# A graph-attention layer on one core: matches of ring places from squared distances in place of turned one-hot matrices

## The chip, the cores and the metric

The kernel runs on 1 core of one Trainium2 chip. The time is the device time of one execution in microseconds (us), the median of several runs. Within the core TensorE (PE; PEld is its weight load), VectorE (DVE), ScalarE (ACT) and GpSimd (POOL) work beside each other, each in the order of its own program, and meet through semaphores; SyncE (SP) issues most DMA transfers. A trailing q (DVEq, POOLq) names an engine's sequencer.

## The reference

12500 nodes of 128 numbers, 212500 edges with 64 numbers each, sorted by destination; 4 heads of 32 numbers.

```python
h = relu(layernorm(x)); n = (h @ W_node.T).reshape(12500, 4, 32)
e = (edge_attr_64 @ W_edge.T).reshape(212500, 4, 32)
att = sum(concat([n[src], n[dst], e], -1) * a, -1)      # edge x head
att = where(att > 0, att, 0.2 * att)
m = maximum(segment_max(att, dst), 0.0)
ex = exp(att - m[dst])
denom = segment_sum(ex, dst) + (212500 - deg)[:, None] * exp(-m)
out = x + segment_sum((ex / denom[dst])[:, :, None] * n[src], dst)
```

## The kernel before

**Prologue.** TensorE turns and projects the node rows (98 windows of 128 nodes); ScalarE writes the projected rows and the source score of each head, 132 numbers a node, to the table `h_table` in memory (`rows_out`, stored by SP's `store_rows`). `s2`, the destination score, stays in SBUF. The gathers of the first 5 groups fetch raw node rows instead (also shown as L487), so that work starts before the table is complete. VectorE then makes flags of where the destination changes from edge to edge (L611), and tables that say for each step which two neighbouring windows its edges fall into (up to L698): `base`, `in_this`, `in_next`, `keep`, and the records from which each engine reads its addresses at run time (`dve_rec`, `act_rec`, `sp_rec`).

**Main loop.** 52 supers of 4 groups of 1024 edges (8 tiles of 128). `walk` (L87) runs a pair of steps twice for each super, so a step is a group. For each super POOL issues 32 indirect gathers (L487) of 128 table rows each, 4 supers ahead in a ring `gath` of 16 slots. A super's first group waits for `released` (DVE, L870: the super four back is done with), and each of its other groups for `stepped` (DVE, L850), which counts finished steps.

The destinations of a step lie within 256 nodes, and `ring` maps them to 128 ring places. A step k takes:

1. DVE: sum of the destination scores (L791), scores with slope (L796 to L814), then `one_hot` of step k+1 (L727: edges on partitions, 1 where the edge's destination is at that ring place, 8 tiles of 128x128 in bf16), then `normalise` (L880 to L886) and the weighted rows `vals` (L835).
2. ACT: exponentials of the maxima before (L1055, L1056), of the scores (L1036, L1037), two small blocks of live scores (`live_s2`, L1078), `transposed` (L1084), `factors` (L1063), `widened` (L1090: the one-hot to f32).
3. PE, `turn_one_hot` of step k+1 (L1210): 8 transposes of `onehot_b` into the bank `bank_t`, started by DVE's L727. ACT's `transposed` copies the bank to `onehot_t` (places on partitions), and PE's `spread_s2` (L1220) multiplies `onehot_t` with the live scores: every edge of step k+1 gets its destination's score, which L791 of step k+1 adds up.
4. PE, the products of step k (L1243): 8 tiles of one-hot times `vals`, f32, shown as 16 matmuls. The next step's `merge` on DVE (L755 to L764) takes them up, then ACT's `factors` and DVE's `rescale` (L772, L775), which ends with `stepped`.

Beside that, PE makes the edge scores of the next super behind the products of a super's second step (`both_products`, L1185, 32 matmuls). Around the fourth step: DVE `z_columns` (L708), PE `turn_z` (L1193), two scans on DVE (L715, L719) for the maximum of each destination, PE `maxima` (L1203), and two copies by ACT (L1014, L1021), for which the next super's L791 waits.

In the rest of the text S is `spread_s2`, T `turn_one_hot`, P the products, Z `both_products`, each with its step's number where one is meant.

What sets the order is the program of each engine alone; there is no scheduler. The lines that wait on PE before S and P:

```python
wait(e, s_sl, count); wait(e, s_sn, count); wait(e, s_e, count)   # spread_s2: live scores, transposed
wait(e, s_v, s_1); wait(e, s_mc, s_1); wait(e, s_de, s_1); wait(e, s_of, s_1)   # products: vals, exp, widened
```

## Time and profile before

| what | value |
|---|---|
| median of 3 runs | 2956.02 us (2949.07 to 2960.83) |
| the profiled execution, its own time | 2958.49 us |
| its span in the trace | 2956.7 us |
| mean granted TensorE clock | 0.618 of full speed |
| PE, DVE, ACT, POOL busy | 1394.2, 1558.5, 796.3, 1576.9 us |
| DMA | 224.74 MB, mean 76 GB/s |

No engine is busy for much over half of the span. The busy times are sums over stages, so the waits by stage have to be read: `<-DVEq L850` behind a POOL row says that a gather started when DVE's sequencer reached L850, `<-remote` that the releasing event isn't among the records of the engines' own instructions, or came later than the modelled end of the instruction that gave it. The record of a TensorE group gives where its matmuls began and a modelled end; when others learnt of that end is seen in the row of the engine that waited.

### The profile page before, as it was taken

To read this page: it belongs to the slowest core of one execution; us is meant where nothing else is said; L and a number is where in the kernel's file an instruction comes from. 1 tells how busy PE (TensorE), PEld (TensorE's weight loads), DVE (VectorE), ACT (ScalarE), POOL (GpSimd) and SP (SyncE) were. 2 spreads that over 40 slices of the span, in tenths; PEclk is the share of its full clock that TensorE was granted. 3 is DMA by queue.
4 is the path that set the end of the run, shared out by engine and by line. 5 is a ranking of instruction groups with operands and counts; after the bars stand their busy time and mean duration, and the time that the engine had idled before them with its cause. 6 is when DMAs were issued, how large, how long until landed. Compare 5 with 4: busy or idle time off the path is not lost.

```text
span 2956.7 us, 39019 instructions
## 1 busy us (share of the span) xinstructions
PE 1394.2 (47%) x9599; PEld 1292.3 (44%) x9600; DVE 1558.5 (53%) x4449; ACT 796.3 (27%) x2329; POOL 1576.9 (53%) x1674
## 2 busy tenths in 40 slices
PE   4424544544545445444455464454544544544465
PEld 4414444434445444344344353444433433534455
DVE  4345554554545555545555445455454555454568
ACT  4412222222222222222222222222222222222233
POOL 6525555555555555555655555556555555555530
PEclk7656665656655656656556556565565666565667
DMA  7352322222222223222222232222222222222220
GB/s 210 81 185 64 81 66 63 78 69 64 78 66 80 67 64 80 67 65 78 68 70 73 67 80 67 65 77 69 66 77 65 79 67 65 81 66 64 80 67 22
DMA packets 119885, 224.74 MB, mean 76 GB/s; under 512 B 40373, under 2 KB 80181, under 8 KB 113093
## 3 DMA queue, kind: packets, MB, share of 16 engines
q0 software_dynamic: 53440, 113.99, 16.5%
q1 hardware_dynamic: 65565, 110.07, 11.5%
q10 hardware_dynamic: 848, 0.35, 0.1%
q8 instruction: 10, 0.16, 0.0%
q14 instruction: 22, 0.18, 0.0%
HBM read 180.28 MB, written 43.98 MB: 76 GB/s over the span
## 4 chain that ended last, share of the span: by engine, by line
another core or an unknown queue 38%; DVE 23%; issue 17%; PE 12%; ACT 5%; DVEq 3%; ACTq 1%; DMA 0%; SPq 0%
PE bank_z L1185 5%; DVE vals L835 5%; DVE bank_rn L715 4%; DVE rows_mem L719 3%; PE bank_w L1243 3%; DVE s_sum L791 2%; ACT onehot_bits L1084 2%; PE bank_rn L1203 2%; PE bank_t L1210 1%; DVE lk L804 1%; DVEq L80 1%; ACT s_live L1078 1%; ACTq L80 1%; DVE den L880 1%
## 5 line engine op out<-in xcount | busy, mean ns | idle before, releaser
L487 POOL DMA_INDIRECT gath<-h_table,idx x1621 | 1531.7, 945 | 1260.1 <-issue 458.1
L1084 ACT COPY onehot_bits<-bank_t 128x1024 bf16<-128x1024 bf16 x209 | 211.5, 1012 | 1279.3 <-remote 915.9
L1220 PE MATMUL bank_s<-s_live,onehot_bits 128*128 128x24 bf16 x1672 | 76.1, 179 | 842.4 <-ACT onehot_bits L1084 759.5
L1220 PEld LDWEIGHTS bank_s<-s_live,onehot_bits 128*128 128x128 bf16 x1672 | 61.1, 102 | 891.4 <-issue 891.4
L1243 PE MATMUL bank_p<-vals,onehot 128*128 128x137 f32 x1664 | 404.2, 435 | 0.3
L1243 PEld LDWEIGHTS bank_p<-vals,onehot 128*128 128x128 f32 x1664 | 377.4, 328 | 4.9 <-DVE vals L835 0.2
L1210 PE MATMUL bank_t<-ident_b,onehot_bits 128*128 128x128 bf16 x1672 | 199.2, 293 | 358.6 <-DVE onehot_bits L727 310.6
L1210 PEld LDWEIGHTS bank_t<-ident_b,onehot_bits 128*128 128x128 bf16 x1672 | 163.5, 139 | 381.9 <-DVE onehot_bits L727 325.3
L1243 PE MATMUL bank_w<-vals,onehot 128*128 128x137 f32 x1664 | 320.8, 367 | 0.0
L1243 PEld LDWEIGHTS bank_w<-vals,onehot 128*128 128x128 f32 x1664 | 298.4, 266 | 0.0
L727 DVE SCALAR_TENSOR_TENSOR onehot_bits<-bank_w,tables,zz 128x1024 bf16 (+1 forms) x209 | 268.3, 1284 | 27.4 <-issue 12.9
L1185 PEld LDWEIGHTS bank_z<-w_edge_bd,ef 128*128 128x128 f32 x1664 | 266.6, 254 | 20.8 <-issue 11.7
L1185 PE MATMUL bank_z<-w_edge_bd,ef 128*128 128x8 f32 x1664 | 261.6, 298 | 21.1 <-issue 12.3
L772 DVE SCALAR_TENSOR_TENSOR live<-live,tables,ab 128x132 f32<-128x132 f32 x209 | 73.3, 351 | 335.8 <-ACT ab L1063 335.8
L755 DVE SCALAR_TENSOR_TENSOR m_run<-m_run,tables,bank_p 128x4 f32<-128x4 f32 x104 | 20.7, 199 | 420.8 <-remote 420.8
L715 DVE TENSOR_TENSOR_SCAN bank_rn<-flag_rows,bank_rn 16x1024 f32<-16x1024 bf16 x52 | 118.7, 2282 | 210.3 <-remote 206.3
L1090 ACT CAST onehot<-onehot_bits 128x1024 f32<-128x1024 bf16 x208 | 214.6, 1032 | 0.0
L791 DVE TENSOR_REDUCE s_sum<-bank_s 128x32 f32<-128x192 f32 x208 | 73.3, 352 | 196.2 <-remote 128.1
L1203 PE MATMUL bank_rn<-ident,rows_mem 16*128 16x16 f32 x416 | 50.1, 256 | 213.9 <-DVE rows_mem L719 213.9
L1063 ACT ACTIVATE ab<-ab_log 128x8 f32<-128x8 f32 x209 | 44.0, 210 | 392.3 <-DVE ab_log L762 380.3
L1203 PEld LDWEIGHTS bank_rn<-ident,rows_mem 16*128 16x128 f32 x416 | 46.0, 206 | 223.2 <-issue 223.2
L835 DVE TENSOR_TENSOR vals<-gath,bank_p 128x1024 f32<-128x1024 f32 x104 | 126.3, 1215 | 0.0
(167 smaller groups left out, 1851.2 us busy)
## 6 DMA issues: line engine op xcount, KB each, us to landing
ef<-in_edges SPq DMA_DIRECT2D x52, 1024.0 KB
out_x<-x_all SPq DMA_DIRECT2D x210, 128.0 KB
gath<-h_table,idx POOLq DMA_INDIRECT x1621
x_all<-in_x SPq DMA_DIRECT2D x14, 448.0 KB, 6.1
out_x<-x_all SPq DMA_DIRECT2D x14, 448.0 KB
h_table<-gath SPq DMA_DIRECT2D x12, 462.0 KB
resets<-ef SPq DMA_DIRECT2D x8, 416.0 KB
flag_rows<-resets SPq DMA_DIRECT2D x52, 64.0 KB
```

What stands on the lines that cost most here:

```text
L487: e.indirect_dma_start(gath[:, q * GPS + g, t * ROW:(t + 1) * ROW], None, table, bass.IndirectOffsetOnAxis(idx[:, q, g * TILES + t:g * TIL ...
L715: e.tensor_tensor_scan(rows, first_rows, rows, NEG, ALU.add, ALU.max).then_inc(scan_f, 1)
L727: e.scalar_tensor_tensor(out=onehot_b[buf][:, :, :], in0=ring_p[:, bass.ds(offset, P)].rearrange("p (a j) -> p a j", a=1) .to_broadcast([P ...
L791: e.tensor_reduce(s2_sum[:, :].rearrange("p (t h) -> p t h", h=HEADS), s2e[q].rearrange("p (t k h) -> p t h k", k=6, h=HEADS), AX_X, ALU.a ...
L835: e.tensor_tensor(vh[:, :, :, 0:HD], gath[:, bass.ds(slot, 1), :].rearrange("p a (t c) -> p (a t) c", c=ROW)[:, :, 0:DIM].rearrange("p t ( ...
L1084: e.copy(onehot_t[:, :, :], bank_t[:, :].bitcast(BF16).rearrange("p (t c) -> p t c", c=P)).then_inc(s_e, 1)
L1090: e.copy(onehot[buf][:, :, :], onehot_b[buf][:, :, :]).then_inc(s_of, 1)
L1185: ins = e.matmul(z_edge[:, 2 * k:2 * k + 2, t, :], ef[:, k, t * P:(t + 1) * P], w_edge_bd[:, :], start=True, stop=True)
L1203: ins = e.transpose(z_back[:, t * GH:(t + 1) * GH], z_rows[:, t * P:(t + 1) * P], ident[0:GH, 0:GH])
L1210: ins = e.transpose(bank_t[:, :].bitcast(BF16)[:, t * P:(t + 1) * P], onehot_b[buf][:, t, :], ident_b[:, :])
L1220: ins = e.matmul(s2e[buf][:, t * S2W:(t + 1) * S2W], onehot_t[:, t, :], s2_live[:, :], start=True, stop=True)
L1243: ins = e.matmul(half_p[q], onehot[q][:, t, :], vals[q][:, t, :], start=(t == 0), stop=(t == TILES - 1))
```

## The change

The transposed one-hot of a step is no longer made from the one-hot. For a ring place p and a destination d, both split in two parts (bits 112 and bits 15, `HIGH` and `LOW`), (ph-dh)^2 + (pl-dl)^2 is zero where they match and at least 1 where they don't. `distances` makes this sum as a matmul over 18 rows: `terms_sb` holds for each edge of a super dh^2, dl^2, dh and dl of its four groups (rows 4g to 4g+3) and two rows of ones; `place_sb` holds for each of the four groups' positions 1, 1, -2ph and -2pl, and in the last two rows ph^2 and pl^2. `place_sb` stands in a block of its own for each group, chosen at run time by `sel`; the columns of `terms_sb` by `at`, both read from a new table `pe_rec`. The result fills `bank_t` (128x512, f32) with half of a step's 1024 edges, so each step takes two, `distances(0)` and `distances(1)`, called D0 and D1 here. ACT's `matched(0)` and `matched(1)` (L1205) write `onehot_t` from them as relu(1 - distance), 128x512 each, in place of `transposed`. The one-hot itself (DVE L727) and `widened` stay.

The distances are made two steps ahead: step k's part of the program runs S of step k+1, D0 of k+2, P of k, D1 of k+2. D1 waits until `matched(0)` has emptied the bank; ACT's `matched(1)` waits for D1 and stands ahead of the next step's `den_parts` and exponentials. `turn_z` comes first in the fourth step, and `maxima` and Z come behind D1.

The terms are made in the prologue and kept in memory (`dst_terms`); SP fetches 32 KB of them for each super (`load_terms`, a ring of four) at a super's first pair, and PE waits for them at the start of a super (`d_terms`).

In the prologue the destinations (`dst_rows`, `dst_next`, `dst_here`) are no longer fetched early, but behind the stores of the projected rows, the first of them on SP where SP had it between loads of x and the others on SP where POOL issued them; they arrive as integers and ACT casts them into banks or `dst_f` (8 casts), DVE splits them in bits (2 operations on 104x2048) and ACT makes squares and casts of them (4 operations on 104x2048) which ACT stores by 4 DMAs; two operations set the terms' rows of ones. VectorE makes the place rows at its start (10 small operations; they go to memory and come back by 5 loads) and `pe_rec` (8 more behind the tables). The comparison for the flags is in 3 pieces, the one for `is_last` in 4. The 14 copies of x to the output move ahead of the resets on SP. POOL waits for the stored terms before the gathers of the first turn's last super. `ident_b` is gone.

```diff
 def pair(u, ...):                                     # PE
-                    turn_one_hot(1 - q, s_2)
                     if beside[q][0]:
                         beside[q][0]()
-                    spread_s2(1 - q, s_2)
+                    spread_s2(1 - q, s_2, (h4, h6)[q])
+                    ahead = (sel_a, at_a) if q == 0 else (sel_b, at_b)
+                    distances(0, *ahead)
...
                     ins.then_inc(s_b, 1)
+                    distances(1, *ahead, (h5, h7)[q])
...
-                ins = e.transpose(bank_t[:, :].bitcast(BF16)[:, t * P:(t + 1) * P],
-                                  onehot_b[buf][:, t, :], ident_b[:, :])
-            ins.then_inc(s_t, 1)
+            def distances(k, sel, at, count=None):
+                if count is not None:
+                    wait(e, s_e, count)
+                e.matmul(bank_t[:, :], place_sb[:, bass.ds(sel, P)],
+                         terms_sb[:, bass.ds(at + k * 512, 512)], start=True, stop=True
+                         ).then_inc(s_t, 1)
...
             def beside(b):
-                return ((None, None, None),
+                return ((lambda: e.wait_ge(d_terms, b * 16 + 16), None, None),
...
 def pair(u, ...):                                     # ACT
                     live_s2((w_b, w_c)[q], s + 3)
-                    transposed(s_2)
+                    matched(0, (h5, h7)[q])
                     factors(s, s_1)
                     widened(1 - q, s, s_2)
+                    matched(1, (h6, h8)[q])
...
-                e.copy(onehot_t[:, :, :], bank_t[:, :].bitcast(BF16).rearrange(
-                    "p (t c) -> p t c", c=P)).then_inc(s_e, 1)
+                e.activation(onehot_t[:, k * 4:(k + 1) * 4, :], bank_t[:, :].rearrange(
+                    "p (t c) -> p t c", c=P), ACT.Relu, bias=one[:, :], scale=-1.0
+                    ).then_inc(s_e, 1)
...
 SP, prologue
-                if c == 10:
-                    e.dma_start(dst_rows, dst_groups).then_inc(d_rows, 16)
...
+            e.dma_start(dst_rows, dst_groups).then_inc(d_rows, 16)
+            e.dma_start(dst_next, dst_l[:, 1, :, :]).then_inc(d_dst, 16)
+            e.wait_ge(d_store, 16 * CHUNKS)
+            wait(e, n_s2, 2)
+            e.dma_start(dst_here, dst_l[:, 0, :, :]).then_inc(d_dst, 16)
...
 POOL, first gathers
-                if g == 1:
-                    e.dma_start(dst_f[:, :, :], dst_l[:, 0, :, :]).then_inc(d_dst, 16)
-                    e.dma_start(dst_next, dst_l[:, 1, :, :]).then_inc(d_dst, 16)
...
             for q in range(1, RING):
+                if q == RING - 1:
+                    e.wait_ge(d_terms_out, 16 * TERMS)
...
 ACT, prologue
+            for bank, g, at, n in turned_rows:
+                e.copy(bank[0:GROUPS // 2, 0:n], dst_rows[:, g, at:at + n]).then_inc(n_turned, 1)
...
+            e.copy(dst_f[:, :, :], dst_here).then_inc(n_turned, 1)
...
+            wait(e, n_bits, 2)
+            for k, (part, func) in enumerate(((dst_rows, ACT.Square), (dst_low, ACT.Square),
+                                              (dst_rows, ACT.Copy), (dst_low, ACT.Copy))):
+                e.activation(terms_out[k], part, func).then_inc(n_terms, 1)
+            wait(e, n_terms, TERMS)
+            for k in range(TERMS):
+                e.dma_start(terms[:, k, :].rearrange("(p g) e -> p g e", g=2), terms_out[k]
+                            ).then_inc(d_terms_out, 16)
```

TensorE in the loop over supers, first pair of a super, in the kernel before (L1210 is T, L1220 S, L1243 P, L1185 Z):

```order
L1210 MATMUL bank_t<-ident_b,onehot_bits 128x128 x8
L1220 MATMUL bank_s<-s_live,onehot_bits 128x24 x8
L282 REGISTER_ALU
L1243 MATMUL bank_p<-vals,onehot 128x137 x8
L282 REGISTER_ALU
L1210 MATMUL bank_t<-ident_b,onehot_bits 128x128 x8
L1220 MATMUL bank_s<-s_live,onehot_bits 128x24 x8
L1243 MATMUL bank_w<-vals,onehot 128x137 x8
L1182 ISA
L282 REGISTER_ALU
L1185 MATMUL bank_z<-w_edge_bd,ef 128x2x4 x16
```

And the same place of the changed kernel (L1346 is S, L1336 D0 and D1, L1377 P, L1310 Z):

```order
L1346 MATMUL bank_s<-s_live,onehot_bits 128x24 x8
L1336 ISA
L1336 MATMUL bank_t<-rows_mem,place_mem 128x512
L305 REGISTER_ALU
L1377 MATMUL bank_p<-vals,onehot 128x137 x8
L305 REGISTER_ALU
L1336 ISA
L1336 MATMUL bank_t<-rows_mem,place_mem 128x512
L305 REGISTER_ALU x2
L1346 MATMUL bank_s<-s_live,onehot_bits 128x24 x8
L1336 ISA
L1336 MATMUL bank_t<-rows_mem,place_mem 128x512
```

The 8 transposes ahead of S are gone; one matmul stands between S and P, and one behind P, where S of the next step follows.

ScalarE at the end of a pair's first step, before (L1078 is `live_s2`, L1084 `transposed`, L1063 `factors`, L1090 `widened`, L1055 and L1056 `den_parts`, L1036 the next step's exponentials):

```order
L1078 ACTIVATE s_live<-s,tables 128x12
L282 REGISTER_ALU
L1084 COPY onehot_bits<-bank_t 128x1024
L1063 ACTIVATE ab<-ab_log 128x8
L1090 CAST onehot<-onehot_bits 128x1024
L1055 ACTIVATE unseen<-m_run 128x4
L1056 ACTIVATE others<-live 128x1
L1036 ACTIVATE bank_w<-dd 128x32
```

And of the changed kernel (L1205 is `matched`, L1183 `factors`, L1212 `widened`):

```order
L1198 ACTIVATE s_live<-s,tables 128x12
L305 ISA
L1205 ACTIVATE onehot_bits<-bank_t,one 128x512
L1183 ACTIVATE ab<-ab_log 128x8
L305 REGISTER_ALU
L1212 CAST onehot<-onehot_bits 128x1024
L305 REGISTER_ALU
L1205 ACTIVATE onehot_bits<-bank_t,one 128x512
L1175 ACTIVATE unseen<-m_run 128x4
L1176 ACTIVATE others<-live 128x1
L1155 ACTIVATE bank_w<-dd 128x32
```

The copy is split in two, and the second half stands behind `widened` and ahead of all that belongs to the next step.

## Rows read from the trace of the kernel before

**Rows 1.** The page: busy time by engine; the chain that ended last.

```profile
PE 1394.2 (47%) x9599; PEld 1292.3 (44%) x9600; DVE 1558.5 (53%) x4449; ACT 796.3 (27%) x2329; POOL 1576.9 (53%) x1674
...
another core or an unknown queue 38%; DVE 23%; issue 17%; PE 12%; ACT 5%; DVEq 3%; ACTq 1%; DMA 0%; SPq 0%
```

**Rows 2.** POOL's waits by releaser, 223.72 to 2844.25: total, times, longest.

```profile
POOL gath L487 <- DVEq L850: 437.8, 96, 8.8
POOL gath L487 <- DVEq L870: 285.3, 48, 8.0
```

**Rows 3.** Windows: us, busy by engine (instructions), PE clock, DMA share, GB/s.

```profile
1025.28:1050.03 24.75, 7.24 (x51) 6.42 (x52) 12.07 (x39) 7.31 (x20) 15.08 (x16) 0.50 0.23 56
1050.03:1063.64 13.61, 8.64 (x65) 8.35 (x65) 5.93 (x19) 3.23 (x13) 7.54 (x8) 0.63 0.30 60
1063.64:1079.90 16.26, 9.73 (x64) 9.00 (x62) 10.18 (x22) 3.49 (x12) 7.55 (x9) 0.71 0.31 99
223.72:2844.25 2620.53, 1240.21 (x8545) 1150.69 (x8544) 1365.32 (x3831) 679.85 (x1990) 1464.28 (x1552) 0.61 0.27 71
2858.39:2890.75 32.36, 21.82 (x176) 20.17 (x176) 27.94 (x80) 14.14 (x41) 0.00 (x0) 0.71 0.15 51
```

**Rows 4.** Timeline 1024 to 1051: start, us, engine, operation, [idle before <-releaser].

```profile
1030.42 0.37 PE L1220 MATMUL bank_s<-s_live,onehot_bits 128*128 128x24 bf16 x8 [1.19 <-issue]
...
1030.75 3.99 PE L1243 MATMUL bank_p<-vals,onehot 128*128 128x137 f32 x16
...
1034.49 0.36 DVE L791 TENSOR_REDUCE s_sum<-bank_s 128x32 f32<-128x192 f32 x1 [2.94 <-remote]
...
1037.46 1.03 PE L1210 MATMUL bank_t<-ident_b,onehot_bits 128*128 128x128 bf16 x8 [2.71 <-DVE onehot_bits L727]
...
1043.99 0.94 POOL L487 DMA_INDIRECT gath<-h_table,idx  x1 [0.30 <-issue]
1048.02 1.01 ACT L1084 COPY onehot_bits<-bank_t 128x1024 bf16<-128x1024 bf16 x1 [11.47 <-remote]
1048.04 0.22 DVE L755 SCALAR_TENSOR_TENSOR m_run<-m_run,tables,bank_p 128x4 f32<-128x4 f32 x1 [8.84 <-remote]
```

**Rows 5.** Timeline 1050 to 1064: the run of eight gathers behind the edge products.

```profile
1053.19 3.75 PE L1185 MATMUL bank_z<-w_edge_bd,ef 128*128 128x8 f32 x32
...
1058.87 0.94 POOL L487 DMA_INDIRECT gath<-h_table,idx  x1 [0.30 <-issue]
1061.63 1.01 ACT L1084 COPY onehot_bits<-bank_t 128x1024 bf16<-128x1024 bf16 x1 [9.87 <-remote]
...
1063.64 0.94 POOL L487 DMA_INDIRECT gath<-h_table,idx  x1 [3.83 <-DVEq L850]
```

**Rows 6.** Timeline 1062 to 1082: the step with the scans.

```profile
1067.44 1.04 PE L1193 MATMUL bank_rn<-ident,z_cols 128*16 128x128 f32 x8
...
1072.98 2.28 DVE L715 TENSOR_TENSOR_SCAN bank_rn<-flag_rows,bank_rn 16x1024 f32<-16x1024 bf16 x1 [4.94 <-remote]
...
1079.90 0.36 DVE L791 TENSOR_REDUCE s_sum<-bank_s 128x32 f32<-128x192 f32 x1 [0.77 <-ACT zz L1021]
```

**Rows 7.** Timeline 2857 to 2872: a step of the tail, with no gathers issued.

```profile
2861.86 1.21 DVE L835 TENSOR_TENSOR vals<-gath,bank_p 128x1024 f32<-128x1024 f32 x1
...
2863.54 0.37 PE L1220 MATMUL bank_s<-s_live,onehot_bits 128*128 128x24 bf16 x8 [1.19 <-ACT onehot_bits L1084]
...
2864.56 0.35 DVE L791 TENSOR_REDUCE s_sum<-bank_s 128x32 f32<-128x192 f32 x1
```

**Rows 8.** Groups of 0 to 216 us: count, busy, mean ns, idle before.

```profile
L975 ACT ACTIVATE ef<-bank_w 128x512 f32<-128x512 f32 x13 | 7.9, 630 | 15.4 <-remote 11.7 <-PE bank_w L1137 3.7
```

**Rows 9.** Timeline 160 to 216: the prologue's last gather, flags, the first restart.

```profile
164.65 0.94 POOL L487 DMA_INDIRECT gath<-h_table,idx  x1 [0.30 <-issue]
...
173.20 2.29 DVE L611 TENSOR_TENSOR ef<-rows_mem 104x2046 bf16<-104x2046 int32 x1 [56.70 <-remote]
...
205.36 0.94 POOL L487 DMA_INDIRECT gath<-h_table,idx  x1 [39.77 <-DVEq L698]
```

More of the change, by code:

```diff
@@ L515, in _ @@
             chain(e.memset(eps[:, :], 4.0 * EPS))
+            chain(e.memset(one[:, :], 1.0))
+            e.memset(place_sb, 0.0).then_inc(n_place, 1)
+            chain(e.memset(place_row[:, 0:2, :], 1.0))
+            wait(e, n_const, 2)
+            chain(e.tensor_copy(place_high, ring[32:33, 0:P]))
+            chain(e.tensor_single_scalar(place_low, place_high, LOW, op=ALU.bitwise_and))
+            chain(e.tensor_single_scalar(place_high, place_high, HIGH, op=ALU.bitwise_and))
+            for k, part in enumerate((place_high, place_low)):
+                times, square = place_row[:, 2 + k, :], place_row[:, TERMS + k, :]
+                chain(e.tensor_scalar(times, part, -2.0, None, ALU.mult))
+                ins = e.scalar_tensor_tensor(out=square, in0=times, scalar=0.25, in1=times,
+                                             op0=ALU.mult, op1=ALU.mult)
+                if k == 0:
+                    chain(ins)
+            ins.then_inc(n_place, 1)
             def statistics(c):
```

171 lines of the change are left out of this document (135 added, 36 removed).

## The prediction

> **What bounds the kernel now.** I read the busy times first: no engine is busy for more than 53% of the span [rows 1], and the chain that ended last puts 38% on events that no record explains. So waits bound it. Who waits? The only engine whose rate gives a floor for the loop is POOL: a gather each 1.25 us (0.94 and 0.30 between [rows 4]), 32 to a super, 40 us. The loop takes longer: 1552 gathers in 2620.53 us [rows 3] are 48.5 supers of 54.03 us. POOL waits in it for DVE's L850 (437.8 us) and L870 (285.3 us) [rows 2], 14.9 us a super. The remaining question is why DVE is late.
>
> A super has three phases, one to each run of gathers: 24.75 us with 16, 13.61 with 8, and a third with 8 that takes 54.03 - 24.75 - 13.61 = 15.67 us in the mean (the one shown 16.26) [rows 3]. In the tail, where no gathers are issued, four steps take 32.36 us with the same matmuls [rows 3]. A single hand-over shows the same: S is issued at 2863.54 and DVE uses it at 2864.56, 1.0 us later [rows 7]; under gathers S(1) is issued at 1030.42 and used at 1034.49, 4.1 us later [rows 4]. P(1), issued at 1030.75 with a modelled length of 3.99, is seen by DVE's L755 only at 1048.04, after 8.84 us idle, and T(2), issued at 1037.46, by ACT at 1048.02 after 11.47 idle [rows 4]: two groups issued 7 us apart come free together, 4.0 us after the start of the run's last gather (1043.99), 22.7 us after the run's first. In the run of 8, Z and T come free at 1061.63, 2.8 us after the last gather (1058.87), 11.6 after the first [rows 5]. Then ACT and DVE work for 2.0 us until POOL's next gather at 1050.03 and at 1063.64. So **the kernel is a loop: a run of gathers holds back TensorE's completions, and these hold back the next run.** Within a run matmuls come back slowly: S(1)'s 8 took 4.07 us, 0.51 each. P(1)'s 16 were not back 13.55 us after S(1), so at least 0.85 each, if they weren't simply held to the end.
>
> Here a rule speaks against my reading. The Trainium skill, "SBUF — State Buffer", section "Who interferes with whom", says that DMA never contends with a compute engine and that TensorE never waits on anyone, having ports of its own. By it the lateness would be TensorE's own. The two ends at a fixed distance from the last gather speak against it; it has a rival below.
>
> **The change, part by part.** PE has 176 matmuls a super [rows 3] (32 S, 32 T, 64 P, 32 Z, 8 `turn_z`, 8 `maxima`); T goes, and 8 D come: 152. In the tail T costs the path little (S, not T, is waited for), so what counts is where T stood in a run.
>
> *Phase 1.* P(1) no longer stands behind T and S, which were made a step earlier; it needs `vals`(1) alone, so I put it 4.85 us after the run's start instead of 5.47. P(1) and D1(3) are 17 matmuls. At 0.51 each they are back at 13.5, at 0.85 at 19.3; I take 0.85, since P is the like of P. Behind D1(3) stand in ACT's order `matched(1)` (0.63, the 128x512 activation [rows 8]), the exponentials of step 2 (two of about 0.2, as the small operations of rows 4) and `live_s2`; for these waits DVE's `vals` (1.21 [rows 7]), and for that PE's P(2) and DVE's `merge`. With D1(3) at 19.3, `vals` ends at 22. Then S(3) and D0(4), 9 matmuls, are issued after 20 and held to the run's end, 22.7. From there before: copy 1.01, then `factors` and `rescale`, 1.0 more, 24.75. Now the copy is a `matched(0)` of 0.63: **24.35, -0.4**.
>
> *Phase 2.* S(4) and D0(5) are held to the end of the run behind Z (32 matmuls) as T was. `matched(0)` for the copy, and S needs no turn through T: 13.1, **-0.5**.
>
> *Phase 3.* Before, `turn_z` is issued at 1067.44 behind T, and the first scan starts at 1072.98 after 4.94 idle, 9.34 us into the run; L791 of the next super follows 6.92 later, and POOL 16.26 after the run's start [rows 6]. T's 8 matmuls are gone from in front of it: at 0.45 each, a little under S(1)'s 0.51, 3.6 us, so the scan starts at 5.7. Floor for this term: none of it, if all is held to the end. With the scan at 5.7 the scans are over at 10.3. Now the next thing is late: P(4) and D1(6), ahead of `maxima`, come at the run's end, 11.5. `maxima` and ACT's copies took what the two scans leave of the 6.92, 6.92 - 2 x 2.28 = 2.4, of which I take 2.0, since the hand-over from the scan is long past and `matched(1)` lies beside `maxima`: 13.5 against 15.67, **-2.2** (0 to -2.8).
>
> Sum -3.1 us a super, times 48.5: **-150 us**.
>
> *The other edits of the loop.* PE's load of `pe_rec` twice a super, has no row; PE idles 1.19 us ahead of S with its present loads [rows 4], which bounds one load, and it lies in PE's wait for `vals`: 0, and if that cover is gone up to 1 us a super. SP's 32 KB a super stand in SP's queue ahead of nothing urgent (DMA is busy 0.27 of the time [rows 3]); PE waits for terms fetched a super ahead: nothing. ACT does two activations of 0.63 for one copy of 1.01, +0.25 a step, in an engine that idles over 8 us in each phase: nothing beyond what stands above.
>
> *Prologue.* The last gather of the first batch starts at 164.65, L611 starts at 173.20 after 56.7 us idle, and POOL starts again at 205.36 with 39.77 idle, released by the last table's operation [rows 9]. What lies on these 32 us is added in full: the casts of `dst_rows` ahead of the flags (3 casts, 1.0 + 0.6 + 0.6 by the length of 128x512 at 0.63 [rows 8]), 2 bitwise operations of 104x2048 at L611's 2.29 [rows 9], 8 small ones at 0.2 for `pe_rec`, some sequencing: 2.2 + 4.6 + 1.6 + 1.2 = 9.6, taken as **+10**. Bounds: 0, if the casts were done before ACT's work is waited for, and +20, if the fetch of `dst_rows` behind the row stores lands late, since nothing hides a DMA there. The first super's distances wait for terms that ACT makes in 4 operations of about 2.3 and stores: beside POOL's gathers of the second and third super, 70 us, for which the new wait of POOL comes too late to matter. The 14 copies of x, now ahead of the resets on SP, may put 0 to 3 us on them.
>
> *Tail.* Without gathers the path loses the T that hid anyway and gains the order P(k), D1, `matched(1)`, exponentials of k+1, which puts P on the path to the next exponentials: 0 to 3 us a super, three supers: **+2**.
>
> Sum: -150 + 10 + 2 = -138. 2958.49 - 138 = 2820.5; the median of before lies 2.5 below its profiled execution: **2818 us**. Own range 2780 to 2900 (phase 3 between half and all of its term, a gain of 1 us in phase 1, prologue to +20).
>
> **The rivals.**
> 1. *No change.* D1(3) is held to the end of run 1 like T(2) was. This is so if matmuls come back at over (22.7 - 4.85)/17 = 1.05 us each. Then all of step 2's exponentials, `vals` and `merge` come after 22.7: matched(1) 0.6, exponentials and waits 0.7, `vals` 1.2, merge, factors, rescale 1.6: 26.8, +2.1. Phase 2 -0.3, phase 3 -2.1: -0.3 x 48.5 + 12 = -3: **2953 us**. For it: P(1) did come exactly with T(2) [rows 4]. Against: S(1) came within the run.
> 2. *Slower.* The same, and `turn_z` isn't earlier either: it is held to 9.3 whatever stands before it, and `matched(1)` adds 0.6 there. +2.1 - 0.3 + 0.6 = +2.4 x 48.5 + 12 = +128: **3084 us**. It decides from the point where P's 16 matmuls and D1 outlast the run: the wait on D1 turns P, which was beside the next step's exponentials, into what they wait for.
> 3. *Faster.* All in the run comes back at S(1)'s 0.51: P(1) and D1(3) at 13.5, S(3) out at 15.0, with D0(4) back at 19.6, POOL's release at 21.2: -3.6; phase 2 -0.5, phase 3 -2.8: -6.9 x 48.5 + 12 = -323: **2633 us**. Against: the 13.55 us of P(1).
> 4. *Lateness is TensorE's own*, by the count of matmuls, not by gathers: 24 of 176 fewer, 14% of POOL's 723 us of waits: -100 + 10: **2866 us**. Against it stands the tail, where the same matmuls are prompt. The Trainium skill's rule named above would lead to this case.
>
> **How the numbers follow.** Main 0.40, no change 0.20, slower 0.20, faster 0.10, TensorE's own 0.10. About 0.5% is what a measurement of this kernel can tell from no change (2941 to 2971). Faster: main, faster and own lateness 0.60, less 0.05 for the main case's weak end, plus 0.05 from the no-change case's spread: 0.60. Within: 0.05 + 0.12 = 0.17. Slower: 0.20 + 0.03 = 0.23. The range goes from 2700, which takes in part of the faster case, to 3010, for the mild part of the slower one (+0.6 to +2.4 a super): it leaves out some 0.06 below and 0.13 above.
>
> **What would show it.** Right, if in the changed kernel the first scan (L715 of before) starts some 6 us into its run rather than 9.3, and the third phase lasts 13.5; if D1(3)'s `matched(1)` comes at most 20 us into the run of 16, and that phase lasts 24.4; if POOL restarts after the prologue at 213 to 218. Wrong, if `matched(1)` of the run of 16 starts at its end, 22.7 (rivals 1 and 2), or if the grouping of gathers in runs of 16, 8 and 8 changes: another grouping makes each phase's sum void. The prices rest on one super's rows, and above all on what P's matmuls do inside a run, which the trace of before bounds only from below.

## The result, and the profile after

| what | before | changed |
|---|---|---|
| median of 17 runs | 2964.85 us | 2990.5 us |
| range of the runs | 2949.07 to 2974.17 | 2950.83 to 3024.38 |
| the profiled execution | 2958.49 us | 3013.91 us |

The ratio of the compared runs is 1.0053 (95% interval 1.003 to 1.0076): slower by half a percent, where 5% faster was forecast. It leaves out, as slow, the 7 of the changed kernel's 17 runs that lie over 1.5% above its fastest; the medians of all runs are 0.9% apart. The changed kernel's runs spread far more than those of before, and its profiled execution lies 23 us above its median; so I take from this trace how it works, and split the time by a pair of traces from one other chip, below.

The page of the changed kernel (busy times; the chain; two groups, with busy and mean ns, then idle time before them and its releaser):

```profile
PE 1497.7 (50%) x8347; PEld 1259.0 (42%) x8348; DVE 1566.5 (52%) x4473; ACT 888.7 (30%) x2554; POOL 1572.2 (52%) x1672
...
another core or an unknown queue 43%; PE 20%; issue 15%; DVE 10%; ACT 7%; ACTq 3%; DVEq 2%; DMA 0%; POOL 0%; SPq 0%; POOLq 0%
...
L1205 ACT ACTIVATE onehot_bits<-bank_t,one 128x512 bf16<-128x512 f32 x420 | 288.5, 687 | 1749.7 <-remote 1211.9
...
L804 DVE TENSOR_TENSOR_SCAN bank_rn<-flag_mem,bank_rn 16x1024 f32<-16x1024 bf16 x52 | 118.4, 2277 | 3.1 <-issue 2.8
```

The same scan's line on the page of the kernel before:

```profile
L715 DVE TENSOR_TENSOR_SCAN bank_rn<-flag_rows,bank_rn 16x1024 f32<-16x1024 bf16 x52 | 118.7, 2282 | 210.3 <-remote 206.3
```

VectorE stood idle ahead of a super's first scan (L804, L715 of before), for `turn_z`, 210.3 us in all in the kernel before; here 3.1 us are left. That is the gain that the change was to bring, and it is there. But more of the chain lies in events that no record explains (43% for 38%, [rows 1]), and ScalarE idles 1749.7 us ahead of `matched` (L1205), 1211.9 of them for an event past the modelled end of TensorE's distances, the only thing that `matched` waits for.

The run of 16 gathers, the same place in a super as [rows 4], which began with a gather at 1112.12 (L1377 is P, L1336 D0 or D1, L1205 `matched`, L1155 the exponentials, L924 `vals`, L1346 S):

```profile
1117.58 3.58 PE L1377 MATMUL bank_p<-vals,onehot 128*128 128x137 f32 x16 [0.71 <-issue]
...
1119.01 0.35 DVE L880 TENSOR_REDUCE s_sum<-bank_s 128x32 f32<-128x192 f32 x1
...
1121.09 0.39 PE L1336 MATMUL bank_t<-rows_mem,place_mem 18*128 x1
...
1130.84 0.94 POOL L541 DMA_INDIRECT gath<-h_table,idx  x1 [0.30 <-issue]
1134.76 0.69 ACT L1205 ACTIVATE onehot_bits<-bank_t,one 128x512 bf16<-128x512 f32 x1 [15.41 <-remote]
...
1135.53 0.19 ACT L1155 ACTIVATE bank_w<-dd 128x32 f32<-128x32 f32 x1
...
1136.46 1.22 DVE L924 TENSOR_TENSOR vals<-gath,bank_w 128x1024 f32<-128x1024 f32 x1
...
1136.49 0.39 PE L1346 MATMUL bank_s<-s_live,onehot_bits 128*128 128x24 bf16 x8 [15.02 <-ACT s_live L1198]
...
1137.45 0.69 ACT L1205 ACTIVATE onehot_bits<-bank_t,one 128x512 bf16<-128x512 f32 x1 [1.19 <-PE bank_t L1336]
...
1139.33 0.94 POOL L541 DMA_INDIRECT gath<-h_table,idx  x1 [7.55 <-DVEq L939]
```

P(1) is issued at 1117.58, 5.5 us into the run, and D1(3) behind it at 1121.09. DVE has the scores of step 2 at 1119.01. But `matched(1)` starts at 1134.76, after 15.41 us idle: 22.6 us into the run and 3.9 behind the start of its last gather. Only then come the exponentials of step 2, `vals` at 1136.46, S(3), `matched(0)`, `factors`, and the next gather at 1139.33. It is the usual case: in 46 of this trace's 49 runs of 16, `matched(1)` starts 22.6 to 22.7 us after the run's first gather. In the kernel before, VectorE had been past `vals` of step 2 and idle for 8.84 us at this point [rows 4], and 2.0 us led from the run's end to the next gather; now it is 4.6.

Windows of the changed kernel: that run, the run of 8 behind it, and a super of the tail (columns as in [rows 3]):

```profile
1112.12:1139.33 27.21, 7.34 (x42) 5.85 (x43) 11.76 (x39) 7.86 (x23) 15.09 (x16) 0.56 0.21 53
1139.33:1152.62 13.29, 12.12 (x70) 10.62 (x69) 6.11 (x20) 3.60 (x13) 7.55 (x9) 0.63 0.25 57
2900.23:2936.62 36.39, 24.52 (x152) 20.21 (x152) 28.17 (x79) 15.39 (x45) 0.00 (x0) 0.73 0.14 47
```

27.21 us against 24.75, and the super without gathers takes 36.39 against 32.36 [rows 3]. The runs don't follow each other as before, either: the gathers of two supers often come as runs of 16, 8, 16, 8, 8 and 8 where they came as 16, 8, 8 and again 16, 8, 8. Over the whole loop, from the starts of the gathers in either trace: 49 runs of 16 at 27.3 us in the mean (24.8 before) and 97 runs of 8 at 13.6 (14.7 before), so +122 us and -101 us. The mean of the runs of 8 hides three different things:

| runs of 8 | before | changed |
|---|---|---|
| with a super's first scan | 48 at 15.6 us | 48 at 12.2 us |
| others | 48 at 13.6 us | 33 at 13.4 us |
| others, over 17 us long | none | 15 at 18.7 us |

The scan starts 8.7 us into its run in the mean before, and 5.0 us in the changed kernel. All 15 long runs follow a run with a scan, as this one does:

```profile
1041.38 0.96 POOL L541 DMA_INDIRECT gath<-h_table,idx  x1 [3.42 <-DVEq L939]
...
1045.69 2.28 DVE L804 TENSOR_TENSOR_SCAN bank_rn<-flag_mem,bank_rn 16x1024 f32<-16x1024 bf16 x1
...
1052.67 0.94 POOL L541 DMA_INDIRECT gath<-h_table,idx  x1 [1.60 <-issue]
...
1071.59 0.94 POOL L541 DMA_INDIRECT gath<-h_table,idx  x1 [9.23 <-DVEq L939]
```

The scan's run takes 11.3 us, from 1041.38 to 1052.67, and the next 18.9 us, after which GpSimd waits 9.23 us for a finished step. So the runs with the scan gain 3.4 us each, 165 us in all, and the 15 long ones cost some 76 us of it.

### The profile page after: what moved, and what is told of

It is laid out like the page before. It is cut to its first block, busy times and chain, and to the rows that moved or that the text cites. A ratio compares the mean times of both kernels' runs of the same rounds, so it can differ in the third digit from the quotient of the medians.

```text
span 3012.1 us, 38483 instructions
## 1 busy us (share of the span) xinstructions
PE 1497.7 (50%) x8347; PEld 1259.0 (42%) x8348; DVE 1566.5 (52%) x4473; ACT 888.7 (30%) x2554; POOL 1572.2 (52%) x1672
## 3 DMA queue, kind: packets, MB, share of 16 engines
q1 hardware_dynamic: 67561, 113.48, 11.4%
## 4 chain that ended last, share of the span: by engine, by line
another core or an unknown queue 43%; PE 20%; issue 15%; DVE 10%; ACT 7%; ACTq 3%; DVEq 2%; DMA 0%; POOL 0%; SPq 0%; POOLq 0%
PE bank_p L1377 7%; PE bank_z L1310 5%; DVE vals L924 4%; PE bank_w L1377 4%; PE bank_t L1336 2%; ACT onehot_bits L1205 2%; ACTq L84 2%; ACT s_live L1198 1%; DVE den L969 1%; ACT unseen L1175 1%; DVE bank_rn L804 1%; DVE den L973 1%; ACT others L1176 1%; DVEq L84 1%
## 5 line engine op out<-in xcount | busy, mean ns | idle before, releaser
L1205 ACT ACTIVATE onehot_bits<-bank_t,one 128x512 bf16<-128x512 f32 x420 | 288.5, 687 | 1749.7 <-remote 1211.9
L1346 PE MATMUL bank_s<-s_live,onehot_bits 128*128 128x24 bf16 x1672 | 79.0, 181 | 948.5 <-ACT s_live L1198 831.1
L1346 PEld LDWEIGHTS bank_s<-s_live,onehot_bits 128*128 128x128 bf16 x1672 | 68.5, 107 | 988.3 <-issue 986.3
L969 DVE SCALAR_TENSOR_TENSOR den<-unseen,others,live 128x4 f32<-128x4 f32 x210 | 47.1, 224 | 788.8 <-ACT others L1176 717.2
L1377 PE MATMUL bank_p<-vals,onehot 128*128 128x137 f32 x1664 | 412.3, 437 | 41.2 <-issue 21.8
L1377 PEld LDWEIGHTS bank_p<-vals,onehot 128*128 128x128 f32 x1664 | 378.9, 327 | 95.3 <-issue 51.1
L1310 PE MATMUL bank_z<-w_edge_bd,ef 128*128 128x8 f32 x1664 | 304.2, 314 | 187.7 <-issue 176.9
L1310 PEld LDWEIGHTS bank_z<-w_edge_bd,ef 128*128 128x128 f32 x1664 | 309.5, 280 | 193.5 <-issue 182.9
L1377 PE MATMUL bank_w<-vals,onehot 128*128 128x137 f32 x1664 | 357.8, 396 | 40.2 <-DVE vals L924 29.7
L1377 PEld LDWEIGHTS bank_w<-vals,onehot 128*128 128x128 f32 x1664 | 332.3, 292 | 81.2 <-DVE vals L924 57.8
L1336 PE MATMUL bank_t<-rows_mem,place_mem 18*128 x420 | 217.7, 518 | 87.2 <-ACT onehot_bits L1205 74.1
L1212 ACT CAST onehot<-onehot_bits 128x1024 f32<-128x1024 bf16 x208 | 216.8, 1043 | 0.6 <-issue 0.2
L924 DVE TENSOR_TENSOR vals<-gath,bank_p 128x1024 f32<-128x1024 f32 x104 | 126.3, 1215 | 0.0
L924 DVE TENSOR_TENSOR vals<-gath,bank_w 128x1024 f32<-128x1024 f32 x104 | 126.3, 1215 | 0.0
L804 DVE TENSOR_TENSOR_SCAN bank_rn<-flag_mem,bank_rn 16x1024 f32<-16x1024 bf16 x52 | 118.4, 2277 | 3.1 <-issue 2.8
L808 DVE TENSOR_TENSOR_SCAN rows_mem<-flag_mem,bank_rn 16x1024 f32<-16x1024 bf16 x52 | 118.3, 2276 | 1.8
L1198 ACT ACTIVATE s_live<-s,tables 128x12 bf16 x418 | 101.2, 290 | 0.3 <-issue 0.3
L1336 PEld LDWEIGHTS bank_t<-rows_mem,place_mem 18*128 x420 | 40.0, 95 | 137.8 <-issue 123.3
```

The source lines that it names most:

```text
L804: e.tensor_tensor_scan(rows, first_rows, rows, NEG, ALU.add, ALU.max).then_inc(scan_f, 1)
L808: e.tensor_tensor_scan(z_rows[:, ::-1], flag_rows[:, 1, ::-1], rows[:, ::-1], NEG, ALU.add, ALU.max).then_inc(scan_b, 1)
L924: e.tensor_tensor(vh[:, :, :, 0:HD], gath[:, bass.ds(slot, 1), :].rearrange("p a (t c) -> p (a t) c", c=ROW)[:, :, 0:DIM].rearrange("p t ( ...
L1198: e.activation(s2_live[:, k * 3 * HEADS:(k + 1) * 3 * HEADS], s2[:, bass.ds(w + k, 1), :].rearrange("p a c -> p (a c)"), ACT.Copy, scale=h ...
L1205: e.activation(onehot_t[:, k * 4:(k + 1) * 4, :], bank_t[:, :].rearrange("p (t c) -> p t c", c=P), ACT.Relu, bias=one[:, :], scale=-1.0).t ...
L1212: e.copy(onehot[buf][:, :, :], onehot_b[buf][:, :, :]).then_inc(s_of, 1)
```

## Experiments

"Chip" below says on which of five chips a kernel ran; the kernel before ran beside each kernel on it. That turned out to matter more than the change: where TensorE's completions come late during gathers (the late kind: the runs of the result, chips 6 and 14) the kernel before takes 2965 to 3073 us, and where they don't (the prompt kind: chips 0, 2 and 5) 2142 to 2147. Each chip ran at one time only, chip 14 at two, so that it is the chip which decides, and not the time, isn't shown.

### Where D1 stands

```diff
                     distances(0, *ahead)
+                    distances(1, *ahead, (h5, h7)[q])      # d1_ahead
...
                     ins.then_inc(s_b, 1)                    # products
-                    distances(1, *ahead, (h5, h7)[q])
```

> The changed kernel with D1 of step k+2 issued right behind D0 of step k+2 and ahead of the products P of step k (TensorE then waits for matched(0) before P). ScalarE's order is as in the changed kernel. Theory A (the exponentials of step 2 wait, through matched(1), for a D1 that stands behind P(1) and is held to the run's end): the run of 16 gathers goes from 27.3 us back to about 24.8, runs of 8 stay at 13.6 in the mean, a super takes about 52 us, and the time is some 110 us under the changed kernel, about 2885. Rival B (the longer run comes from the distances themselves or from ScalarE's two activations, wherever D1 stands): the run of 16 stays at 27.3 and the time within 0.5% of the changed kernel's.

> The changed kernel with D1 ahead of P, once more. Where the kernel before takes about 2146: 2146 again, since GpSimd's issue of 1661 gathers at 1.25 us sets the end. Where it takes about 2960 theory A (exponentials behind D1 behind P) gives runs of 16 gathers of 24.8 us instead of 27.3 and about 2885; rival B gives 27.3 and 2980.

> The changed kernel with D1 ahead of P, once more, in the hope of a chip on which completions are held back during gathers, as on the one of the profile shown and on the one where the kernel before took 3072. There theory A: runs of 16 gathers of about 24.8 us instead of 27.3, runs of 8 as in the changed kernel (13.6 in the mean), ratio to the kernel before 0.97 to 0.98. Rival B: 27.3 us and a ratio of 1.00 to 1.01. On a chip with prompt completions: 1.001.

And in ScalarE's order alone (`m1_behind`):

```diff
                     live_s2((w_b, w_c)[q], s + 3)
+                    matched(1, (h4, h6)[q])
                     matched(0, (h5, h7)[q])
                     factors(s, s_1)
                     widened(1 - q, s, s_2)
-                    matched(1, (h6, h8)[q])
...
             matched(0, 3)                                   # ahead of the loop
-            matched(1, 4)
```

> The changed kernel with one edit in ScalarE's order alone: matched(1) of step k+2 moves from the end of step k's part to behind the exponentials and live_s2 of step k+1. D1 still stands behind P. Theory A: exponentials and vals of step 2 are done during the run; but D1(3), then S(3) and D0(4) still come one after another from the run's end on, so only the 0.9 us of the exponentials and live scores leave the path: the run of 16 takes about 26.4, the time is some 45 us under the changed kernel. If the exponentials alone mattered, the run of 16 would go back to 24.8 (-120 us). Rival B: no change.

> ScalarE's order alone changed: matched(1) of step k+2 behind the exponentials and live_s2 of step k+1; D1 still behind P. Where completions are held back: if the exponentials and vals behind D1 are the whole loss, the run of 16 goes from 27.3 to 24.8 us and the time to that of d1_ahead, 3% under the kernel before. If the chain D1(3), matched(1), S(3), D0(4), matched(0), factors from the run's end on is the rest of it, the run of 16 takes about 26.4 and the time is about 1.5% under the changed kernel's.

The first runs were on chips on which the kernel before takes 2146 and 2142 us, not 2965. There the two gave 1.0002 (0.9993 to 1.0012) and 0.9995 (0.9986 to 1.0005), both on chip 5, and `d1_ahead_b` on chip 0 gave 1.0016 (1.0006 to 1.0026). On two other chips the kernel before takes 3068 to 3073 us, and there:

| kernel | chip | before | this | ratio (95%) | runs of 16, of 8 |
|---|---|---|---|---|---|
| changed | 6 | 3072.8 | 3063.9 | 0.9979 (0.996 to 0.9998) | 27.7, 13.9 us |
| m1_behind | 6 | 3072.8 | 2985.4 | 0.9724 (0.9699 to 0.9748) | 26.9, 13.6 us |
| d1_ahead | 14 | 3067.8 | 2971.0 | 0.9677 (0.9657 to 0.9696) | 25.1, 13.7 us |
| before | 6 | | | | 25.1, 15.7 us |

`d1_ahead_c`, the run of 16 from 724.80 on (L1378 is P here):

```profile
724.80 0.94 POOL L541 DMA_INDIRECT gath<-h_table,idx  x1 [6.05 <-DVEq L959]
...
734.27 0.60 PE L1336 MATMUL bank_t<-rows_mem,place_mem 18*128 x1 [2.71 <-ACT onehot_bits L1205]
...
734.80 3.90 PE L1378 MATMUL bank_p<-vals,onehot 128*128 128x137 f32 x16
...
737.01 0.19 ACT L1155 ACTIVATE bank_w<-dd 128x32 f32<-128x32 f32 x1
...
738.56 1.21 DVE L924 TENSOR_TENSOR vals<-gath,bank_w 128x1024 f32<-128x1024 f32 x1
...
747.86 0.22 DVE L844 SCALAR_TENSOR_TENSOR m_run<-m_run,tables,bank_p 128x4 f32<-128x4 f32 x1 [8.09 <-remote]
...
749.61 0.94 POOL L541 DMA_INDIRECT gath<-h_table,idx  x1 [4.82 <-DVEq L939]
```

D1 goes out at 734.27, ahead of P at 734.80. The exponentials of step 2 run at 737.01 and `vals` at 738.56, 13.8 us into the run, while P(1) is still seen only at its end (L844, 23.1 us in, after 8.09 idle); the next gather follows at 24.8. So theory A holds for the run of 16: the 2.6 us by which it was longer were the exponentials and what follows them, behind a D1 that stood behind P. `m1_behind` takes only the exponentials out and leaves D1(3), S(3), D0(4) in a row behind the run's end: 0.9 us of the 2.6 come back (26.9; 26.4 was expected).

The times don't follow from the runs of 16 alone. `m1_behind` is 78.5 us or 2.6% under the changed kernel on the same chip, where 45 us or 1.5% was expected: 43 us come from its 49 runs of 16, some 30 from its 97 runs of 8 and 12 from behind the last gather. So ScalarE's order alone, with D1 still behind P, gives back most of what `d1_ahead` does (0.9724 and 0.9677, on two chips). And `d1_ahead` makes another pattern: 165 runs of 8, of 10.4 to 19.0 us, and only 15 of 16. Why the runs regroup wasn't followed up; the changed kernel itself didn't run on chip 14.

### The same on purpose: products four times over

```diff
-                    for t in range(TILES):
+                    for t in list(range(TILES)) * 4:
                         ins = e.matmul(half_p[q], onehot[q][:, t, :], vals[q][:, t, :],
```

> The kernel before with every step's products P made four times over (64 matmuls instead of 16, the last pass counts): late products built by hand, on a chip where completions are otherwise prompt. P of a step lies beside the exponentials and vals of the next step, so TensorE sets the pace: four P (8.5 us at full clock, 16 at half) and some 2 us of T and S a step, 11 to 18 us a step, 2300 to 3700 us. Serves as the base for the next two.

> The changed kernel with the same fourfold P. Theory A (exponentials of the next step stand, through matched(1) and D1, behind P): TensorE waits after every P for D1, matched(1), exponentials and vals, some 3 us a step, so 208 steps cost about 500 to 650 us more than longp_before. Rival B (D1's place doesn't matter): the same as longp_before or up to 150 us less, since 24 of 176 matmuls a super are gone.

> The changed kernel with D1 ahead of P and the same fourfold P. Theory A: the exponentials are free of P again, and the time is that of longp_before or up to 150 us under it. Rival B: as longp_after.

Chip 14: 3756.2, 3904.5 and 3687.1 us. `longp_before` was meant for a chip of the prompt kind, and chip 14 is of the late one. The order of the three is theory A's: D1 behind P costs 217 us over D1 ahead of it. The size was wrong: +148 us for the changed kernel, 0.7 us a step and not 3. That the gathers had slowed P to where it hid much of the chain would explain it, and isn't shown.

### The prologue

> The prologue, memory layout and fetches of the changed kernel (terms are made, stored and fetched, place rows are made), with the loop of the kernel before: eight transposes, one copy, no distances. Theory: the prologue alone costs what the traces show, GpSimd's restart at 228 us instead of 205, so +22 us or +0.8% over the kernel before, with runs of 24.8 and 14.7 us as before. Rival: the loop's fetches of terms or the new place of the rows slow the loop too: runs of gathers longer than before. Rival: the later restart is made up for behind it: no change against before.

> The changed kernel's prologue and fetches with the loop of the kernel before. Where completions are held back: GpSimd restarts at 228 us instead of 205 and the loop is that of the kernel before, so +22 us, 0.7 to 0.8%. Rivals: the fetches of terms lengthen the loop (more than 1%); the delay is made up (0%). Where completions are prompt: 1.000, as before.

```diff
 flags_early
-            for bank, g, at, n in turned_rows:
-                e.tensor_tensor(inner[:, g, at:at + n], bank[0:GROUPS // 2, 0:n],
-                                dst_rows[:, g, at + 1:at + 1 + n], ALU.not_equal
+            e.tensor_tensor(inner, dst_rows[:, :, 0:GROUP - 1], dst_rows[:, :, 1:GROUP],
```

> The changed kernel with one part undone: dst_rows is loaded early as in the kernel before (between loads of x) and compared by one VectorE operation straight from the integers, without the three casts by ScalarE. Theory: the flags waited for ScalarE's last projected rows, 10.6 us of the later restart; they start some 8.5 us after the last gather of the first batch again instead of 19.1, and the restart comes 8 to 10 us earlier (218 to 220): -0.3% against the changed kernel. Rival: the casts of dst_here and dst_next, which also wait for those rows, are next and keep the restart at 226 or later.

> The changed kernel with D1 ahead of P, the flags' load and comparison as in the kernel before (flags_early), and the ten small operations for the place rows moved behind VectorE's first four chunks. Where completions are held back: d1_ahead's gain plus 8 to 10 us of the prologue, ratio to the kernel before 0.963 to 0.966; without the prologue's part 0.968. Where they are prompt: GpSimd's issue sets the end, 0.999 to 1.002.

`prologue_only` gave 0.9993 (0.9984 to 1.0003) on chip 5, where +22 us was expected at first, and 1.0073 (1.0055 to 1.009) on chip 6, +22 us. The second number is the expected one, but its reason isn't shown: in the trace on chip 6 GpSimd restarts at 225.7 us, against 215.6 in the kernel before, and not at 228 against 205. So the later restart explains 10 us, and 12 stay open; the trace is also that of the fastest of its four runs, 11 us under their median. On chip 5 the reason is in GpSimd's waits (engine, line, releaser: us in all, times, longest):

```profile
POOL gath L542 <- issue: 493.4, 1619, 0.3
...
POOL gath L542 <- DMA h_table<-onehot: 8.4, 1, 8.4
```

Its waits are its own issue gaps, and one wait of 8.4 us for the stored table: GpSimd issues almost without a stop from 68 us to 2096 us, at 1.25 us a gather, and whatever happens behind it costs nothing. `flags_early` gave 1.0049 (1.0033 to 1.0066) there; with no restart to wait for, it couldn't answer its question, and it was slower. `combo` ran on such a chip too (chip 2): 0.9997 (0.9988 to 1.0006). What the flags' part is worth where completions are late stays open.

### The kernels themselves on one chip

> The kernel before as it is, for its trace on the same chip as the others of this call. Where completions are held back: runs of 16 and 8 gathers again, 24.8 and about 14.7 us or longer. Where they are prompt: GpSimd issues back to back, 2142 to 2146 us.

> The changed kernel as it is. Where completions are held back: runs of 16 at 27.3 us, runs of 8 at 13.6, 0 to 1% over the kernel before. Where they are prompt: +0.4%.

> The changed kernel as it is, beside the kernel before on the same chip. In the first runs of this study the kernel before took 2146 us with GpSimd issuing gathers back to back, where the profile shown had taken 2958 with GpSimd waiting for TensorE's late completions. Theory H (the gain and the loss of the change lie only where completions are held back during gathers): where the kernel before takes about 2146, this one does too, within 0.2%; where it takes about 2960, this one takes 0.5% more. Rival: the distances' longer ScalarE and TensorE chain costs time of its own: slower than before by over 0.5% where completions are prompt.

`after_b` (chip 0): 2149.8 against 2141.9 us, 1.0038 (1.0024 to 1.0052), more than theory H's 0.2% and less than its rival's 0.5%. Behind the last gather it takes 53.5 us, and 47.8 with D1 ahead of P (`d1_ahead_b`), so 5.7 of the 7.9 us may lie there; the kernel before has no trace on that chip. On chip 6 the traces of both kernels split the time. GpSimd's waits in the loop, the kernel before:

```profile
POOL gath L487 <- DVEq L850: 462.0, 97, 9.4
...
POOL gath L487 <- DVEq L870: 375.2, 48, 8.9
```

and the changed one (L939 is L850 of before, L959 is L870, and in the rows below L787 is L698):

```profile
POOL gath L541 <- DVEq L939: 655.4, 98, 9.8
...
POOL gath L541 <- DVEq L959: 108.9, 28, 4.3
```

Waits for a finished step grew by 193 us, waits for a finished super fell by 266. In three stretches: restart of the gathers 215.6 and 226.7 us (+11.1), from there to the last gather 2754.4 and 2712.1 (-42.3; of it 49 runs of 16 at +2.6 and 97 runs of 8 at -1.8), behind it 107.3 and 121.8 (+14.6). Sum -16.6, as the spans: 3077.2 and 3060.6. The medians are only 8.9 us apart, since the profiled execution of the kernel before lies 6.3 above its median. The prologue in rows, before:

```profile
169.54 0.94 POOL L487 DMA_INDIRECT gath<-h_table,idx  x1 [0.30 <-issue]
...
183.44 2.29 DVE L611 TENSOR_TENSOR ef<-rows_mem 104x2046 bf16<-104x2046 int32 x1 [23.36 <-PE bank_rn L1153]
...
215.60 0.94 POOL L487 DMA_INDIRECT gath<-h_table,idx  x1 [45.12 <-DVEq L698]
```

changed (L1076 the last projected rows, L1091 the first cast, L682 the flags):

```profile
173.10 0.94 POOL L541 DMA_INDIRECT gath<-h_table,idx  x1 [0.30 <-issue]
...
185.77 0.63 ACT L1076 ACTIVATE gath<-bank_rn,zz 128x132 f32<-128x132 f32 x2
186.44 1.01 ACT L1091 CAST bank_rn<-rows_mem 104x1023 f32<-104x1023 int32 x1
...
188.62 1.22 DVE L682 TENSOR_TENSOR ef<-bank_rn,rows_mem 104x1023 bf16<-104x1023 f32 x1 [35.37 <-ACT bank_s L1091]
...
226.72 0.94 POOL L541 DMA_INDIRECT gath<-h_table,idx  x1 [52.68 <-DVEq L787]
```

The second batch of gathers ends 3.6 us later (it waits for the stored table, behind a VectorE that began about 2 us later); the flags start 15.5 instead of 13.9 us behind it, and only behind ScalarE's last rows; from the flags to the restart it takes 38.1 instead of 32.2.

### Fewer gathers, fewer products

```diff
 half_gathers_before, half_gathers_after: behind the first turn of the ring
-                    for t in range(LAST_TILES if last else TILES):
+                    for t in range(0, LAST_TILES if last else TILES, 2):
 half_p
-                    for t in range(TILES):
+                    for t in range(TILES // 2):
                         ins = e.matmul(half_p[q], onehot[q][:, t, :], vals[q][:, t, :],
```

> The kernel before with every other gather of the loop left out after the first ring (4 of 8 tiles a group; the rest of the rows are stale). Lateness by gathers: where completions are held back, runs of 4 and 8 gathers end at 1.4 us a gather, and a super takes about 40 instead of 54 to 56 us; lateness of TensorE's own: a super stays over 50. Where completions are prompt the compute chain sets the pace: 32.4 us a super as in the tail, 1750 us.

> The changed kernel with the same gathers left out. Where completions are prompt: the chain P, D1, matched(1), exponentials, vals is serial and costs 4.0 us a super (36.4 against 32.4 in the two tails), so 200 us or 11% more than half_gathers_before, which GpSimd's issue otherwise hides. Where they are held back: 4 us a super more too, or more.

> The kernel before with half of the products P left out (4 of the 8 tiles of a step, 8 matmuls instead of 16), so half of the edges are missing from the sums. Where completions are held back: if each matmul comes back at its own slow rate (0.85 to 1.05 us), P(1) is seen by DVE's L755 14 to 18 us into the run of 16 gathers; if what is issued in the middle of a run is held to its end whatever its size, at 22.8 us as in the kernel before, and the runs keep their lengths of 25.1 and 15.7. Where completions are prompt it tells nothing (2142 us).

All three ran on chip 2, where completions are prompt. `half_p` (2146.4 us) tells nothing there, as its expectation says. The other pair shows the chain without GpSimd's issue over it: 1733.3 and 2054.9 us, +322 us or 6.2 us a super, where 4.0 was expected. A step of `half_gathers_after` (L1339 D1, L1208 `matched(1)`, L1158 exponentials, L927 `vals`, L1380 P):

```profile
1003.71 0.41 PE L1339 MATMUL bank_t<-rows_mem,place_mem 18*128 x1
...
1004.15 0.69 ACT L1208 ACTIVATE onehot_bits<-bank_t,one 128x512 bf16<-128x512 f32 x1 [2.57 <-PE bank_t L1339]
...
1004.92 0.19 ACT L1158 ACTIVATE bank_w<-dd 128x32 f32<-128x32 f32 x1
...
1005.85 1.21 DVE L927 TENSOR_TENSOR vals<-gath,bank_w 128x1024 f32<-128x1024 f32 x1
...
1007.12 3.80 PE L1380 MATMUL bank_w<-vals,onehot 128*128 128x137 f32 x16 [0.56 <-DVE vals L927]
```

D1 behind the last P at 1003.71, `matched(1)` 1004.15, exponentials 1004.92, `vals` 1005.85, the next P at 1007.12: 3.4 us in which TensorE makes nothing but D1, S, D0 and here `turn_z`. In the kernel before this lay beside P. Its mean granted clock is lower as well, 0.67 of full speed against 0.78 for `half_gathers_before` (600 to 1600 us), and TensorE is busy for 25.6 us a super against 20.2, with fewer matmuls. So the 6.2 us are the serial order and the lower clock together, and these two runs don't part them.

## Why the prediction was wrong, point by point

- **What bounds the kernel: right for these chips.** The loop of gathers and late completions is there in the runs of the result and on chips 6 and 14, and without it, on chips 0, 2 and 5, the same kernel takes 28% to 30% less. The Trainium skill's page "SBUF — State Buffer", section "Who interferes with whom", says that DMA never contends with a compute engine and that TensorE never waits on anyone. The trace of chip 5 agrees with it; on chips 6 and 14 completions are late during gathers, and by what path gathers and TensorE meet there isn't shown. Rival 4, lateness by the count of matmuls, fits badly: the tail of the same trace is prompt with the same matmuls [rows 3], [rows 7], and in `longp_after`, with 64 matmuls to a P, 146 of ScalarE's 184 late waits still end 11.6 to 11.7 us after a run's first gather. Fewer gathers weren't tried on a chip of the late kind.
- **Phase 1: the step that failed.** "At 0.85 each they are back at 19.3; I take 0.85, since P is the like of P." P(1) was issued 5.5 us into the run, not 4.85, and D1(3) was seen at 22.6, at the run's end, so that the next step's exponentials and `vals`, which stand behind `matched(1)`, came after it: the run takes 27.3 us where 24.35 was forecast. That is the run of 16 of rivals 1 and 2 (26.8), each given 0.20, and the time came out between theirs. 0.85 was a lower bound only, taken as the value. The trace of `longp_before`, where P has 64 matmuls, shows how TensorE goes on in such a run (it begins at 1039.18; L1220 is S, L1243 P, L791 waits for S):

```profile
1039.18 0.94 POOL L487 DMA_INDIRECT gath<-h_table,idx  x1 [9.93 <-DVEq L870]
...
1047.57 0.37 PE L1220 MATMUL bank_s<-s_live,onehot_bits 128*128 128x24 bf16 x8 [1.57 <-issue]
...
1047.90 5.21 PE L1243 MATMUL bank_p<-vals,onehot 128*128 128x137 f32 x26
...
1055.69 0.28 PE L1243 MATMUL bank_p<-vals,onehot 128*128 128x137 f32 x1 [2.58 <-issue]
...
1058.50 0.39 PE L1243 MATMUL bank_p<-vals,onehot 128*128 128x137 f32 x1 [2.54 <-issue]
...
1059.92 0.39 PE L1243 MATMUL bank_p<-vals,onehot 128*128 128x137 f32 x1 [1.03 <-issue]
...
1061.32 0.39 PE L1243 MATMUL bank_p<-vals,onehot 128*128 128x137 f32 x1 [1.01 <-issue]
...
1062.01 5.66 PE L1243 MATMUL bank_p<-vals,onehot 128*128 128x137 f32 x34 [0.30 <-issue]
1062.02 0.36 DVE L791 TENSOR_REDUCE s_sum<-bank_s 128x32 f32<-128x192 f32 x1 [13.44 <-remote]
```

S(2) is issued at 1047.57, and VectorE sees it at 1062.02, 14.45 us later. TensorE gets 26 matmuls of P out behind it and then stands, and later starts one each 2.8, 1.4, 1.4 us; from the run's end on (22.8 us in) 34 follow in 5.7 us. So with 64 matmuls to make TensorE starts one each 1.4 to 2.8 us late in a run, not one each 0.85. If matmuls come back at the same rate as it starts them, 17 can't be back within the run. That TensorE stands because its unreported completions are full is my reading, argued and not shown.
- **Phases 2 and 3: the mechanism right, the sizes only in the sum.** The scan's wait for `turn_z` is gone, and the scan starts 5.0 us into its run (5.7 was forecast). Its run takes 12.2 us against the forecast's 13.5: -3.4, outside the stated 0 to -2.8. The ordinary other run takes 13.4 (13.1 was forecast). And 15 runs of 18.7 us are in no term of the sum; the prediction itself had written that another grouping makes each phase's sum void, and the runs did regroup. That the runs of 8 have a mean of 13.6 beside the forecast's 13.3 is two misses that nearly cancel.
- **Prologue: right on one chip, mis-sized on another.** +10 was forecast. The restart of the gathers comes 11.1 us later in the pair of chip 6, 12.8 to 13.7 in the `longp` traces of chip 14, and 22.6 in the traces of the result (228.0 against 205.4). What was missing is the wait of the whole second batch for the stored table, which ends 3.3 us later on chip 6 and 8.2 in the traces of the result. The bitwise operations took 1.22 us, not 2.29.
- **Tail and the serial chain: mis-sized.** "0 to 3 us a super", +2 in all, was 4.0 us a super in the tail and 6.2 in `half_gathers_after`: +11 to +15 us behind the last gather. The order P, D1, `matched(1)`, exponentials was named there, and priced far too low: I had `matched(1)`'s 0.6 in mind and not the whole of what P had covered.
- **Sum.** With phase 1 at +2.5, the tail at +12 and the prologue at +22 in place of -0.4, +2 and +10, and phases 2 and 3 left as they were, my sum gives (2.5 - 2.7) x 48.5 + 22 + 12 = +24 us. The ratio gives +16, and the medians of all runs +26. That it comes so near is partly luck, by the two misses of phases 2 and 3; and on chip 6 the same change measured 0.9979 (0.996 to 0.9998). So the mis-sized phase 1 took back most of the gain or all of it on both chips, and what was left over has another sign on the other chip.

## What to carry to other kernels

Ahead of any move, list what stands behind the new instruction in each engine's order: D1 behind P made P a thing that the next step's exponentials wait for, and that took back what the change gained. With one line moved ahead of P the kernel is 3.2% faster than before on chip 14, and with one activation moved in ScalarE's order 2.8% on chip 6, where the changed kernel as it is gives 0.2%. A time that a trace bounds from one side only is no value: where the sum's sign hangs on it, the case beyond the bound deserves a large chance. A mean over runs that do different things hides misses that cancel. And before a wait is worked on, see whether it is there on another chip.

## What the runs showed of the hardware

- The same kernel takes 2142 to 2147 us on chips 0, 2 and 5, within 0.2% on each of them, and 2965 to 3073 us where the result was taken and on chips 6 and 14. GpSimd issues a gather each 1.25 us on both kinds. On the late kind matmuls issued during gathers are seen up to 17 us after they were issued (P(1) at 1030.75, seen at 1048.04 [rows 4]); on the prompt kind the turned one-hots of a step, issued at 1041.45, are copied from 1042.11 on (`prologue_only`). What holds the completions back, and what differs between the chips, stays open.
- On the late kind what a run of 16 gathers holds back is seen 22.6 to 23.1 us after its first gather (the kernel before and the changed kernel, where the result was taken and on chip 6), with P and T or P and D1 issued, 24 or 17 matmuls; what a run of 8 holds to its end, 11.4 to 11.9 us after it. With a P of 64 matmuls in hand at the end of a run of 16, the 34 that are left are started within 6 us (`longp_before`).
- Where the issue of gathers sets the end, a serial order on TensorE, ScalarE and VectorE that costs 322 us once half of the gathers are gone (chip 2) shows as 0.4% (chip 0).
